# Attention over a graph on one core: PE's semaphores raised by drains instead of matmuls, ScalarE's copies in mid-chain with immediate biases, one-hots behind messages, and gathers up to 14 steps ahead

## The chip, the cores and the metric

The kernel runs on one core of one Trainium2 chip. The metric is the device time of one execution in microseconds (us). The engines are PE (TensorE, matmuls and their weight loads), DVE (VectorE), ACT (ScalarE), POOL (GpSimd, which here issues gathers) and SP (SyncE, which issues the large loads and the stores).

## The reference

One layer of graph attention with a residual and a layer norm. There are 6250 nodes with 128 features, 206250 edges (sorted by receiver) with 128 features each, and 4 heads of 32.

```python
sent  = nodes[senders] @ Ws + Ws_b
e_att = sent + edges @ We + We_b                      # (E, 4, 32)
recv  = nodes[receivers] @ Wr + Wr_b
logits = mish(e_att + recv) @ attn_w + attn_b         # (E, 4)
w = exp(logits - segment_max(logits, receivers)[receivers])
w = w / segment_sum(w, receivers)[receivers]
out = segment_sum(w * e_att, receivers)
x = layernorm(x + out)
```

## The kernel before

The node tables `nodes @ Ws` and `nodes @ Wr` are made first and written to DRAM. Then the edges are worked through in 51 windows of 4096 edges, 32 tiles of 128. A window has 8 groups of 4 tiles; the work on one group is called a step, so there are 408 steps. `run` writes two windows out, loops over pairs of windows, and ends with three more calls, so that each engine has its own fixed program, and only semaphores tie the engines to each other. Each window's softmax and sums are finished during the next two windows, beside those windows' own groups.

For group g of window w:

- POOL gathers the senders' rows of the table by four indirect DMAs (L717), each one tile of 128 rows. Ahead of a group it waits until PE has finished the products of the group `AHEAD` = 4 steps back (semaphore z_ps).
- DVE makes the one-hot matrix of the receivers (`one_hots`, L1113), three steps ahead of the group's products. It waits until PE has finished the sums that read the same buffer two windows earlier (sum_ready).
- PE turns (transposes) the edge tiles (L793) and the one-hot tiles (L798) into PSUM, two steps ahead (`turn`). The last transpose of each kind raises edgeT_ps or onehotT_ps.
- ACT copies both to SBUF (`copy_edgeT` L907, `copy_onehotT` L914).
- PE multiplies (`products`, L815 and L816, 16 matmul records a group) into ps_z; the last one raises z_ps.
- DVE adds the gathered rows (`add_gathered`, L1122), giving Z.
- ACT runs a chain of five activations over Z (`bound` L923, then `ratio_step` L930, L933, L936, L939), each with its bias in a 128x1 tile. From it DVE makes mish times the attention weights, and reduces it to logits (`mish` L1129, `score` L1138, `reduce_heads` L1144), one step later.
- In the window after, DVE finds the maxima over receivers and the weights, and multiplies Z by the weights (`messages`, L1205, at the steps in MSG_NEXT and MSG_LAST). PE sums the messages by receiver (`sums`, L827, 8 matmul records a group, at the steps in SUM_NEXT and SUM_LAST); the last matmul of a group raises sum_ready. Sums of group 0 wait until DVE has read the sums of the window before (att, L1224). `ends_to_row` (L835) and `maxima_back` (L842) are small transposes for the maxima, once a window each.

PE's order within a step is products, turn of the group two ahead, sums of the window before the last, the small transposes, and sums of the last window. ACT's is both copies, then the chain. DVE's is one-hots, Z, messages, and then mish, score and reduce with small operations between them (`aside`).

## Time and profile before

| | |
|---|---|
| median of 3 runs | 2656.48 us (2653.65 to 2662.03) |
| span of the profiled execution | 2661.8 us |
| PE busy | 1917.4 us, 72% |
| DVE busy | 1895.0 us, 71% |
| ACT busy | 1927.7 us, 72% |
| POOL busy | 1575.1 us, 59% |
| mean granted TensorE clock | 0.835 |

The span runs from the first to the last instruction of the profiled execution and is taken as that execution's time; no time of it around the span is on record, and it lies 0.2% above the median. Busy time is the time in which an engine executes; what it waits for is found in the list of waits and in the timelines. A releaser called "remote" is one that the profile can't name. "issue" is time in which the engine waited for nothing that the profile shows. PE's matmul ends are modelled, their starts are recorded. In a merged row of the timeline (x8) the time runs from the first start to the last end.

### The profile page before, as it was taken

The page shows a single profiled execution, that of the slowest core. Times are in us where ns is not written, and L with a number is a line of the kernel's source. Part 1 is how long each engine was busy: PE and PEld are TensorE (multiplying, and loading weights), DVE is VectorE, ACT ScalarE, POOL GpSimd, SP SyncE. Part 2 cuts the span into 40 slices and gives each one's busy share as a digit, 9 for nine tenths or more (in the row PEclk, how much of TensorE's full clock was granted, in tenths as well). Part 3 has the DMA queues.
Part 4 walks back from the last instruction along what each step waited for, and adds up shares of the span by engine and source line. Part 5 has one row for each costly group of instructions (what it writes and reads, how often), then busy time and mean ns, then how long its engine had stood idle before and what let it go on. Part 6 is the DMA issues. An engine that isn't in the chain of part 4 may idle for free.

```text
span 2661.8 us, 45397 instructions
## 1 busy us (share of the span) xinstructions
PE 1917.4 (72%) x13621; PEld 1789.2 (67%) x13621; DVE 1895.0 (71%) x3941; ACT 1927.7 (72%) x3126; POOL 1575.1 (59%) x1640
## 2 busy tenths in 40 slices
PE   5667777777776777776776777776777777776776
PEld 5567666766666776766666766666667676666665
DVE  2676777777777767776676777766777777677766
ACT  1777777777777777777777777777777777777774
POOL 2666656656666665666566656656666666556661
PEclk8888888888888887888888888878888888878877
DMA  6422322322232322232232232232223232223220
GB/s 191 130 77 80 105 83 78 112 79 77 81 111 77 97 96 77 77 113 79 76 112 79 78 105 86 78 100 90 78 93 99 79 98 95 77 86 104 79 79 17
DMA packets 106714, 240.18 MB, mean 90 GB/s; under 512 B 45800, under 2 KB 72546, under 8 KB 99658
## 3 DMA queue, kind: packets, MB, share of 16 engines
q1 hardware_dynamic: 53334, 132.54, 14.6%
q0 software_dynamic: 52224, 107.06, 14.1%
q10 hardware_dynamic: 1128, 0.25, 0.0%
q8 instruction: 13, 0.21, 0.0%
q14 instruction: 15, 0.12, 0.0%
HBM read 229.98 MB, written 9.74 MB: 90 GB/s over the span
## 4 chain that ended last, share of the span: by engine, by line
DVE 36%; PE 20%; another core or an unknown queue 18%; issue 17%; ACT 7%; DVEq 1%; DMA 1%; ACTq 0%; SPq 0%
PE ps_sum L827 7%; DVE Z L1122 6%; DVE tbuf L1138 6%; DVE tbuf L1129 6%; DVE Z L1205 5%; PE ps_z L815 4%; PE ps_z L816 4%; DVE onehot L1113 4%; DVE logit L1144 2%; PE ps_edgeT L793 2%; ACT tbuf L933 1%; ACT tbuf L930 1%; ACT tbuf L936 1%; ACT tbuf L923 1%
## 5 line engine op out<-in xcount | busy, mean ns | idle before, releaser
L717 POOL DMA_INDIRECT landing<-xs_table,src_i x1632 | 1574.2, 965 | 1034.1 <-issue 448.3
L815 PE MATMUL ps_z<-we_sb,edgeT 128*128 128x128 f32 x3264 | 767.2, 320 | 83.3 <-issue 82.4
L816 PE MATMUL ps_z<-xr_buf,onehotT 128*128 128x128 f32 x3264 | 751.9, 315 | 72.3 <-issue 71.5
L827 PE MATMUL ps_sum<-Z,onehot 128*128 128x132 f32 x3264 | 558.9, 321 | 204.7 <-DVE att L1224 95.2
L815 PEld LDWEIGHTS ps_z<-we_sb,edgeT 128*128 128x128 f32 x3264 | 613.0, 232 | 100.9 <-issue 97.3
L816 PEld LDWEIGHTS ps_z<-xr_buf,onehotT 128*128 128x128 f32 x3264 | 609.4, 231 | 83.1 <-issue 82.8
L827 PEld LDWEIGHTS ps_sum<-Z,onehot 128*128 128x128 f32 x3264 | 485.6, 224 | 223.8 <-issue 149.4
L1113 DVE TENSOR_TENSOR onehot<-iota_f,ps_dve 128x512 f32<-128x512 f32 x408 | 276.0, 677 | 432.5 <-remote 352.6
L923 ACT ACTIVATE tbuf<-Z,c_zmax 128x512 f32<-128x512 f32 x408 | 296.2, 726 | 165.7 <-DVE Z L1122 85.9
L907 ACT COPY edgeT<-ps_edgeT 128x512 f32<-128x512 f32 x408 | 235.3, 577 | 229.4 <-remote 179.9
L798 PE MATMUL ps_onehotT<-ident_half,onehot 128*128 128x128 bf16 x1632 | 176.6, 232 | 241.8 <-issue 103.8
L1122 DVE TENSOR_TENSOR Z<-ps_z,landing 128x512 f32<-128x512 f32 x408 | 278.5, 683 | 88.6 <-remote 72.9
L914 ACT CAST onehotT<-ps_onehotT 128x512 f32<-128x512 bf16 x408 | 238.8, 585 | 132.9 <-remote 120.5
L798 PEld LDWEIGHTS ps_onehotT<-ident_half,onehot 128*128 128x128 bf16 x1632 | 125.0, 104 | 291.3 <-issue 226.7
L930 ACT ACTIVATE tbuf<-tbuf,c_zmax 128x512 f32<-128x512 f32 x408 | 294.7, 722 | 13.3
L793 PE MATMUL ps_edgeT<-ident,landing 128*128 128x128 f32 x1632 | 281.1, 295 | 32.3 <-issue 31.9
L933 ACT ACTIVATE tbuf<-tbuf,c_one 128x512 f32<-128x512 f32 x408 | 294.6, 722 | 13.3
L936 ACT ACTIVATE tbuf<-tbuf,c_one 128x512 f32<-128x512 f32 x408 | 294.5, 722 | 13.3
L939 ACT ACTIVATE tbuf<-tbuf,c_ln 128x512 f32<-128x512 f32 x408 | 294.0, 721 | 11.6
L1129 DVE SCALAR_TENSOR_TENSOR tbuf<-tbuf,Z 128x512 f32<-128x512 f32 x408 | 279.3, 685 | 26.6 <-ACT tbuf L939 21.2
L1138 DVE TENSOR_TENSOR tbuf<-tbuf,ps_dve 128x512 f32<-128x512 f32 x408 | 278.4, 682 | 9.0
L1144 DVE TENSOR_REDUCE logit<-tbuf 128x16 f32<-128x512 f32 x408 | 277.9, 681 | 7.3
(110 smaller groups left out, 1228.3 us busy)
## 6 DMA issues: line engine op xcount, KB each, us to landing
landing<-in_edge_attr_dram SPq DMA_DIRECT2D x51, 2048.0 KB
landing<-xs_table,src_i POOLq DMA_INDIRECT x1632
x_in<-in_x_dram SPq DMA_DIRECT2D x51, 64.0 KB
xr_in<-xr_table SPq DMA_DIRECT2D x51, 64.0 KB
out_dram<-y_out SPq DMA_DIRECT2D x51, 64.0 KB
xr_buf<-xr_table SPq DMA_DIRECT2D x50, 64.0 KB
xs_table<-onehot SPq DMA_DIRECT2D x2, 896.0 KB
xr_table<-landing SPq DMA_DIRECT2D x1, 1568.0 KB
```

Source lines behind the costliest of these rows:

```text
L717: nc.gpsimd.indirect_dma_start(gath[b][:, t, :], None, xs_dram, bass.IndirectOffsetOnAxis(ap=src_i[:, b, t:t + 1], axis=0))\
L793: tr = nc.tensor.transpose(ps_edgeT[g % 2][:, j, :], edge_buf[:, b, a + j, :], ident[:, :])
L815: nc.tensor.matmul(ps_z[q][:, j, :], edgeT[:, q, j, :], we_sb[:, :], start=True, stop=False)
L816: mm = nc.tensor.matmul(ps_z[q][:, j, :], onehotT[:, q, j, :], xr_buf[:, b, :], start=False, stop=True)
L827: mm = nc.tensor.matmul(ps_sum[:, 0:ZC], OHv[:, b, t, :], Zv[:, b, t, :], start=(t == 0), stop=(t == T - 1))
L923: nc.scalar.activation(tb, Zv[:, b, a:a + n, 0:D], ACT.Relu, bias=c_zmax[:, 0:1], scale=-1.0)\
L930: nc.scalar.activation(tb, tb, ACT.Exp, bias=c_zmax[:, 0:1], scale=-1.0).then_inc(exp_done, 1)
L1113: nc.vector.tensor_tensor(OHv[:, b, a:a + n, :], iota_f[:, :].unsqueeze(1).to_broadcast([P, n, P]), local[:, b, a:a + n].unsqueeze(2).to_b ...
L1122: nc.vector.tensor_tensor(Zv[:, b, a:a + n, 0:D], ps_z[g % 2][:, 0:n, :], gath[b][:, a:a + n, :], ALU.add).then_inc(z_ready, 1)
L1129: nc.vector.scalar_tensor_tensor(out=tb, in0=tb, scalar=1.0, in1=Zv[:, b, a:a + n, 0:D], op0=ALU.subtract, op1=ALU.mult, reverse0=True)\
L1138: nc.vector.tensor_tensor(tb, tb, row.to_broadcast([P, n, D]), ALU.mult).then_inc(scored, 1)
L1144: nc.vector.tensor_reduce(logit[:, b, :, a:a + n].rearrange("p h t -> p t h"), tb, AX.X, ALU.add)\
```

## The change

PE's matmuls in the windows no longer raise semaphores. After the products of a group and all sums of that step PE executes a drain, and this raises z_ps; sum_ready is raised behind it. Then PE turns the pieces of the group two ahead, and a second drain raises one semaphore, turned_ps, in place of edgeT_ps and onehotT_ps. The small transposes have a drain of their own. The sums thus stand ahead of the turned pieces, and the groups 0 and 1 of the last window are summed in step 5, group 2 in step 6 and group 3 in step 7. ACT does both copies in one place, the one-hots first, behind the third operation of its chain instead of ahead of the first. The activations' biases are immediates instead of 128x1 tiles, and the tile c_zmax is gone. DVE makes its one-hots after Z and the messages of a step instead of first. POOL may gather 14 steps ahead instead of 4. SP waits for turned_ps where it waited for edgeT_ps.

```diff
-AHEAD = 4
+AHEAD = 14
...
-SUM_NEXT = {5: [0], 6: [1], 7: [2, 3]}
+SUM_NEXT = {5: [0, 1], 6: [2], 7: [3]}
...
-                wait_apart(sp, edgeT_ps, at(w - 2, NG - 1), past_sp)
+                wait_apart(sp, turned_ps, at(w - 2, NG - 1), past_sp)
...
                 if g == 0:
                     pe.wait_ge(edge_landed[b], k * 16 + 16)
-                wait(pe, edgeT_ready, at(w, g) - 2)
                 for j in range(n):
-                    tr = nc.tensor.transpose(ps_edgeT[g % 2][:, j, :], edge_buf[:, b, a + j, :], ident[:, :])
-                tr.then_inc(edgeT_ps, 1)
+                    nc.tensor.transpose(ps_edgeT[g % 2][:, j, :], edge_buf[:, b, a + j, :], ident[:, :])
                 pe.wait_ge(onehot_ready, at(w, g))
                 wait(pe, onehotT_ready, at(w, g) - 1)
...
-                tr.then_inc(onehotT_ps, 1)
+                return tr
...
-                mm.then_inc(z_ps, 1)
+                return mm
...
-                mm.then_inc(sum_ready, 1)
+                return mm
...
                 for g in range(NG):
                     if there(w):
                         products(w, b, k, g)
+                    last = SUM_LAST.get(g, []) if there(w - 2) else []
+                    for m in last:
+                        sums(w - 2, b, m)
+                    coming = SUM_NEXT.get(g, []) if there(w - 1) else []
+                    for m in coming:
+                        sums(w - 1, 1 - b, m)
+                    if there(w):
+                        pe.drain().then_inc(z_ps, 1)
+                    elif last or coming:
+                        pe.drain()
+                    if last or coming:
+                        pe.sem_inc(sum_ready, len(last) + len(coming))
                     w1, b1, g1 = two_after(w, b, g)
                     if there(w1) and there(w):
                         turn(w1, b1, k if w1 is w else (k + b if b else k), g1)
-                    for m in SUM_LAST.get(g, []) if there(w - 2) else []:
-                        sums(w - 2, b, m)
+                        pe.drain().then_inc(turned_ps, 1)
...
                     if g == 1 and there(w - 1):
                         ends_to_row(w - 1, 1 - b)
+                        pe.drain().then_inc(ends_ps, 1)
                     if g == 3 and there(w - 1):
                         maxima_back(w - 1)
-                    for m in SUM_NEXT.get(g, []) if there(w - 1) else []:
-                        sums(w - 1, 1 - b, m)
+                        pe.drain().then_inc(back_ps, 1)
...
+            def copy_turned(w, b, g):
+
                 n = GROUPS[g][1]
                 q = g % 2
...
+                act.wait_ge(turned_ps, at(w, g))
                 wait(act, z_ps, at(w, g) - 2)
                 nc.scalar.copy(onehotT[:, q, 0:n, :], ps_onehotT[:, 0:n, :].bitcast(BF16)[:, :, 0:P])\
                     .then_inc(onehotT_ready, 1)
+                nc.scalar.copy(edgeT[:, q, 0:n, :], ps_edgeT[q][:, 0:n, :]).then_inc(edgeT_ready, 1)
...
-                nc.scalar.activation(tb, Zv[:, b, a:a + n, 0:D], ACT.Relu, bias=c_zmax[:, 0:1], scale=-1.0)\
+                nc.scalar.activation(tb, Zv[:, b, a:a + n, 0:D], ACT.Relu, bias=ZMAX, scale=-1.0)\
...
-                    nc.scalar.activation(tb, tb, ACT.Square, bias=c_one[:, 0:1]).then_inc(sq_done, 1)
+                    nc.scalar.activation(tb, tb, ACT.Square, bias=1.0).then_inc(sq_done, 1)
...
-                    if coming:
-                        copy_edgeT(w1, b1, g1)
-                        copy_onehotT(w1, b1, g1)
                     if here:
                         bound(w, b, g)
                         ratio_step(w, g, 0)
                         ratio_step(w, g, 1)
+                    if coming:
+                        copy_turned(w1, b1, g1)
...
-                    if there(w1) and there(w):
-                        one_hots(w1, b1, g1)
                     if there(w):
                         add_gathered(w, b, k, g)
                     if g == 4 and there(w - 1):
                         weights_near(w - 1, 1 - b)
                     all_messages(w, b, g)
+                    if there(w1) and there(w):
+                        one_hots(w1, b1, g1)
```

## Rows read from the trace of the kernel before

**Rows 1.** The page: span, busy time by engine, and the gathers' group (mean ns).

```profile
span 2661.8 us, 45397 instructions
...
PE 1917.4 (72%) x13621; PEld 1789.2 (67%) x13621; DVE 1895.0 (71%) x3941; ACT 1927.7 (72%) x3126; POOL 1575.1 (59%) x1640
...
L717 POOL DMA_INDIRECT landing<-xs_table,src_i x1632 | 1574.2, 965 | 1034.1 <-issue 448.3
```

**Rows 2.** The waits: engine, line, releaser: us in total, times, longest.

```profile
POOL landing L717 <- remote: 364.1, 147, 3.4
DVE onehot L1113 <- remote: 352.6, 104, 9.5
...
POOL landing L717 <- PE ps_z L816: 185.0, 80, 15.4
```

**Rows 3.** The timeline, DVE and PE: steps 4 to 6 of a window, and mid-chain.

```profile
1202.07 0.68 DVE L1122 TENSOR_TENSOR Z<-ps_z,landing 128x512 f32<-128x512 f32 x1
...
1207.05 0.28 DVE L1224 TENSOR_TENSOR att<-ps_sum,rden 128x128 f32<-128x128 f32 x1
...
1207.99 0.17 DVE L1095 TENSOR_SCALAR far<-dst_i 128x32 f32<-128x32 int32 x1
...
1213.13 1.12 PE L827 MATMUL ps_sum<-Z,onehot 128*128 128x132 f32 x8
...
1214.09 0.38 PE L815 MATMUL ps_z<-we_sb,edgeT 128*128 128x128 f32 x2
...
1220.98 0.69 DVE L1113 TENSOR_TENSOR onehot<-iota_f,ps_dve 128x512 f32<-128x512 f32 x1 [6.15 <-remote]
...
1239.31 0.27 PE L816 MATMUL ps_z<-xr_buf,onehotT 128*128 128x128 f32 x1 [2.42 <-issue]
```

**Rows 4.** The timeline of POOL's gathers, and one wait of DVE.

```profile
38.35 1.11 POOL L717 DMA_INDIRECT landing<-xs_table,src_i  x1 [36.61 <-DMA xs_table<-onehot]
...
73.63 0.94 POOL L717 DMA_INDIRECT landing<-xs_table,src_i  x1 [15.45 <-PE ps_z L816]
...
1218.25 0.94 POOL L717 DMA_INDIRECT landing<-xs_table,src_i  x1 [0.30 <-issue]
...
1327.07 0.94 POOL L717 DMA_INDIRECT landing<-xs_table,src_i  x1 [0.30 <-issue]
...
1329.82 0.69 DVE L1113 TENSOR_TENSOR onehot<-iota_f,ps_dve 128x512 f32<-128x512 f32 x1 [6.39 <-remote]
...
2609.04 0.95 POOL L717 DMA_INDIRECT landing<-xs_table,src_i  x1 [0.30 <-issue]
```

**Rows 5.** The timeline of one step without a stall: DVE, PE and weight loads.

```profile
1225.90 0.68 DVE L1122 TENSOR_TENSOR Z<-ps_z,landing 128x512 f32<-128x512 f32 x1
...
1228.68 0.30 PEld L815 LDWEIGHTS ps_z<-we_sb,edgeT 128*128 128x128 f32 x2
...
1228.79 0.38 PE L815 MATMUL ps_z<-we_sb,edgeT 128*128 128x128 f32 x2
...
1229.98 0.68 DVE L1122 TENSOR_TENSOR Z<-ps_z,landing 128x512 f32<-128x512 f32 x1
```

**Rows 6.** Busy time by stretch; after the busy times come granted clock, DMA, GB/s.

```profile
1100.00:1600.00 500.00, 362.30 (x2593) 337.67 (x2592) 359.92 (x747) 369.26 (x602) 305.23 (x316) 0.84 0.28 89
```

**Rows 7.** Groups: busy us, mean ns, idle before; PE's large ones, two of ACT's.

```profile
L815 PE MATMUL ps_z<-we_sb,edgeT 128*128 128x128 f32 x3264 | 767.2, 320 | 83.3 <-issue 82.4
L816 PE MATMUL ps_z<-xr_buf,onehotT 128*128 128x128 f32 x3264 | 751.9, 315 | 72.3 <-issue 71.5
L827 PE MATMUL ps_sum<-Z,onehot 128*128 128x132 f32 x3264 | 558.9, 321 | 204.7 <-DVE att L1224 95.2 <-issue 93.8 <-DVE Z L1205 9.6
L793 PE MATMUL ps_edgeT<-ident,landing 128*128 128x128 f32 x1632 | 281.1, 295 | 32.3 <-issue 31.9
...
L956 ACT ACTIVATE lnv<-mv,c_eps 128x1 f32<-128x1 f32 x51 | 14.3, 280 | 14.7 <-DVE mv L1242 14.7
L958 ACT ACTIVATE rstd<-lnv 128x1 f32<-128x1 f32 x51 | 10.3, 203 | 1.6
```

More of the change, by code:

```diff
@@ L55 @@
 NLATER = 3
-VCONST = 12
-IOTAS = 11
+VCONST = 11
 SEARCH = 3
@@ L157, in gat_kernel @@
         c_eps = sb("c_eps", [P, 1])
-        c_zmax = sb("c_zmax", [P, 1])
         ones = sb("ones", [P, 1])
@@ L257, in gat_kernel @@
         onehot_ready = sem("onehot_ready")
-        edgeT_ps = sem("edgeT_ps")
-        onehotT_ps = sem("onehotT_ps")
+        turned_ps = sem("turned_ps")
         edgeT_ready = sem("edgeT_ready")
@@ L835, in ends_to_row @@
                     tr = nc.tensor.transpose(ps_ends[0:H, c * P:(c + 1) * P], ends, ident[:, :])
-                tr.then_inc(ends_ps, 1)
+                return tr
             def maxima_back(w):
@@ L842, in maxima_back @@
                     tr = nc.tensor.transpose(ps_ends[:, c * H:(c + 1) * H], im[:, c, :], ident[0:H, 0:H])
-                tr.then_inc(back_ps, 1)
+                return tr
             def window(w, b, k):
@@ L857, in window @@
                         ends_to_row(w - 1, 1 - b)
+                        pe.drain().then_inc(ends_ps, 1)
                     if g == 3 and there(w - 1):
                         maxima_back(w - 1)
-                    for m in SUM_NEXT.get(g, []) if there(w - 1) else []:
-                        sums(w - 1, 1 - b, m)
+                        pe.drain().then_inc(back_ps, 1)
             pe.wait_ge(s_xs, 2 * NB)
-            turn(0, 0, 0, 0)
-            turn(0, 0, 0, 1)
+            for g in range(2):
+                turn(0, 0, 0, g)
+                pe.drain().then_inc(turned_ps, 1)
             run(pe, window)
@@ L900, in _ @@
             act.wait_ge(s_vconst, VCONST)
-            def copy_edgeT(w, b, g):
+            def copy_turned(w, b, g):
                 n = GROUPS[g][1]
                 q = g % 2
-                act.wait_ge(edgeT_ps, at(w, g))
-                wait(act, z_ps, at(w, g) - 2)
-                nc.scalar.copy(edgeT[:, q, 0:n, :], ps_edgeT[q][:, 0:n, :]).then_inc(edgeT_ready, 1)
-            def copy_onehotT(w, b, g):
-                n = GROUPS[g][1]
-                q = g % 2
-                act.wait_ge(onehotT_ps, at(w, g))
+                act.wait_ge(turned_ps, at(w, g))
                 wait(act, z_ps, at(w, g) - 2)
@@ L929, in ratio_step @@
                     act.wait_ge(bounded, at(w, g))
-                    nc.scalar.activation(tb, tb, ACT.Exp, bias=c_zmax[:, 0:1], scale=-1.0).then_inc(exp_done, 1)
+                    nc.scalar.activation(tb, tb, ACT.Exp, bias=ZMAX, scale=-1.0).then_inc(exp_done, 1)
                 elif k == 1:
                     act.wait_ge(exp_done, at(w, g))
-                    nc.scalar.activation(tb, tb, ACT.Square, bias=c_one[:, 0:1]).then_inc(sq_done, 1)
+                    nc.scalar.activation(tb, tb, ACT.Square, bias=1.0).then_inc(sq_done, 1)
                 elif k == 2:
                     act.wait_ge(sq_done, at(w, g))
-                    nc.scalar.activation(tb, tb, ACT.Ln, bias=c_one[:, 0:1]).then_inc(ln_done, 1)
+                    nc.scalar.activation(tb, tb, ACT.Ln, bias=1.0).then_inc(ln_done, 1)
                 else:
                     act.wait_ge(ln_done, at(w, g))
-                    nc.scalar.activation(tb, tb, ACT.Exp, bias=c_ln2[:, 0:1], scale=-1.0).then_inc(ratio_ready, 1)
+                    nc.scalar.activation(tb, tb, ACT.Exp, bias=LN2, scale=-1.0).then_inc(ratio_ready, 1)
             def items(w):
@@ L982, in _ @@
             for g in range(2):
-                copy_edgeT(0, 0, g)
-                copy_onehotT(0, 0, g)
+                copy_turned(0, 0, g)
             run(act, window)
@@ L993, in _ @@
             nc.vector.memset(c_eps[:, :], EPS).then_inc(s_vconst, 1)
-            nc.vector.memset(c_zmax[:, :], ZMAX).then_inc(s_vconst, 1)
             nc.vector.memset(ones[:, :], 1.0).then_inc(s_vconst, 1)
```

## Prediction

> **What bounds the kernel now.** I read the page first, then the list of waits, then the timelines of a stalled stretch and of a smooth one, then the groups of PE and ScalarE. The page shows no engine at its limit: DVE, ScalarE and PE lie near 72%, GpSimd at 59% [rows 1]. The span of 2661.8 us holds 408 steps (51 windows of 8), so a step takes about 6.3 us, and no engine has that much work: DVE 1895.0/408 = 4.64 us, ScalarE 1927.7/408 = 4.72 us, and GpSimd four gathers of 965 ns with 0.30 us between two of them [rows 1, 4], 5.06 us. So the order of the work bounds it, not a rate.
>
> The list of waits says which order. The longest ones end at "remote", a releaser that the profile can't place: GpSimd's gathers 364.1 us and DVE's one-hots 352.6 [rows 2]; ScalarE's copies follow. On one core there is no other core. What each of these instructions waits for is, by the code, a semaphore raised by PE's last matmul of a group. The stalled stretch shows it: PE's group of sums starts at 1213.13 and lasts 1.12, the products behind it start at 1214.09; yet the one-hots that wait for sum_ready start at 1220.98, after 6.15 us idle [rows 3]. The signal came some 6 us after the work. When nothing is late, one DVE step takes 1229.98 - 1225.90 = 4.08 us [rows 5].
>
> When are signals late? Between 1218 and 1330 us DVE's one-hots have four such waits. In the first GpSimd's last gather ended at 1219.19 and DVE was let go at 1220.98; in the last they are 1328.01 and 1329.82: 1.8 us after the gathers had stopped both times [rows 3, 4]. GpSimd had stopped because it waits for z_ps, a signal of the same kind. I read this as: signals attached to matmuls are held up while gathers are being issued. That is argued from these places, not shown.
>
> **The change, part by part.**
>
> *The drains.* No matmul of the windows raises a semaphore any more; a drain does, after products with sums, and after the turned pieces. If the drain's signal is prompt, the "remote" waits go. What then sets the time? First GpSimd: it starts at 38.35 and issues 1632 gathers at 965 + 300 ns, the last of them at 38.35 + 1631 x 1.265 = 2101.6; from the last gather's start to the end lie 2661.8 - 2609.04 = 52.8 us [rows 1, 4]. That floor is 2154 us. Second PE: a step has 32 matmuls, 16 of products, 8 of sums, 8 of turned pieces, at 0.11 us from start to start (two in 0.38 us where one lasts 0.27 [rows 3, 5]), 3.52 us, at the mean granted clock of 0.84 [rows 6] 4.19 us. Its idle time put down to "issue" on the four large lines is 82.4 + 71.5 + 93.8 + 31.9 = 280 us [rows 7], 0.69 us a step. The trace has no drain between matmuls. From below, an empty PE costs the last matmul's tail and the next weight load: a lone matmul lasts 0.27 us against 0.11 of spacing, and a load takes 0.19 (two in 0.30) [rows 3, 5], so 0.16 + 0.19 = 0.35 us. From above, a drain waits as long as a late signal does, 3.4 us on average (352.6/104 [rows 2]). I take the lower value, since PE went on starting matmuls while its signal was out, and only the signal is seen to be late. Two drains: 0.70 us. PE's step is then 4.19 + 0.69 + 0.70 = 5.58 us; times 408 = 2277 us, with 73 us up to the first products (they release GpSimd at 73.63 [rows 4]) and 53 behind, 2403 us. This counts every slow-clock stretch of today, while PE should wait less than today.
>
> The Trainium skill (PSUM — Partial Sum Buffer, Engine vs sequencer instructions) tells to attach the increment to the matmul, and says of a drain that it "waits for the engine to go fully idle". By that rule the change gives away PE's overlap twice a step. The trace has no such drain to agree with.
>
> *Sums before the z_ps signal, regrouped.* Z of a step with sums now waits one to two groups of 8 matmuls (0.9 to 1.8 us) longer. DVE has other work until then, but not in the step with groups 0 and 1 (step 5): group 0 waits for att, which DVE makes 5.3 us after Z of step 4 (1202.07 to 1207.33 [rows 3]); two groups and a drain later, 1.8 + 0.35, z_ps comes at 1209.5, where DVE is free at 1208.2. So 1.3 us a window of DVE idle, 3.1 at half clock: 65 to 160 us of DVE in all. Against 5.06 us per step of GpSimd, DVE has 0.42 spare, 3.4 us a window, so it lies beside the gathers as long as these run ahead. Without that cover it costs its 65 to 160 us. What is late next there: the turned pieces of step 7, whose copies ScalarE reaches only behind three activations. SP's load of edges waits for the same drain, under 1 us later, for pieces needed six steps on: nothing.
>
> *ScalarE.* The two copies move from the head of the step behind three activations, so bound starts sooner by both, and PE gets its pieces three activations later, with two steps of lead: nothing by itself. Five activations a step lose their bias tile. With one 128x1 input, ln with a bias tile takes 280 ns and exp without takes 203 [rows 7]: 77 ns, times 5 times 408 = 157 us of ScalarE's busy time, between nothing (if it is the function's difference) and that. ScalarE falls to some 4.34 us a step, and as it was no bound, it gives slack only.
>
> The Trainium skill (ScalarE: Activation LUTs, What ACT_TABLE_LOAD costs) gives about 93 ns for each pointer operand. By it the sum would be 190 us, an estimate from that page; the row's 77 ns is on its side.
>
> *One-hots behind messages.* Three steps ahead as before; 0.6 to 1.9 us later in the step, and PE needs them one step on. Z starts 0.6 us sooner. Nothing is queued behind a late one-hot but mish of the step before, whose ratio is ready later anyway. *Gather lead 14.* Gathers now wait for a step 14 back, so GpSimd stops only for sender indices, which SP loads about two windows ahead. Alone it takes 549 us of GpSimd's waits for z_ps (364.1 + 185.0 [rows 2]) away, which cost nothing now unless Z waits for a landing.
>
> **The sum.** Between GpSimd's 2154 and PE's 2403 I take 2300 us: above the middle (2279), as window edges and step 5 cost a little on either bound, below PE's own sum since the clock should be higher. The page's execution took 2661.8, the median of the runs shown is 2656.48, 0.2% less; 2300 stands for both.
>
> **The rivals.** *Forecast: signals prompt, step 5.0 to 5.8 us.* For it: the stalls hang on signals, not on work, and the "remote" waits are all for PE's. Against: the cause of the delay isn't seen. 2154 to 2450 us, chance 0.62.
>
> *PE becomes the bound and eats most of it.* Drains of 0.5 us: 4.88 + 1.0 = 5.88 us a step, 2399 + 126 = 2525 us. For it, PE stands in mid-chain without a wait for 2.42 us at 1239.31 [rows 3], which no drain mends. Chance 0.13, 2450 to 2640.
>
> *Slower: the hold is on the matmuls' completion, not on the signal.* Then a drain waits for it, PE stands instead of running ahead, and lead 14 removes the pauses in the gathers after which the hold ended. With the 1.8 us of the stalls per drain a step is 4.88 + 3.6 = 8.5 us, some 3590 us. It decides from 0.72 us a drain, where 4.88 + 1.44 is today's 6.3. For it: all stalls ended after a pause. Against: matmuls kept starting every 0.11 us while the signal was out (products from 1214.09 [rows 3]), so results were moving. Chance 0.22.
>
> The Trainium skill (SBUF — State Buffer, Who interferes with whom) has it that PE waits on no one and that DMA doesn't contend with engines. By it the gathers would not be the cause and the lead harmless. The stalls speak against it, without proof.
>
> *No change:* signals stay late but no more often, the lead hides it. 2650 to 2665, chance 0.03.
>
> **How the numbers follow.** No change means within 0.3%, about what a measurement of this kernel can tell. Faster is 0.62 + 0.13 = 0.75, same 0.03, slower 0.22. The range starts at the gather floor, 2150, and reaches to 2700: the forecast, PE as the bound, no change and a few of the slower cases, 0.8 together. The likeliest case's own range is 2154 to 2450.
>
> **What the profile after would show.** Right: hardly any "remote" wait, under 150 us in all; GpSimd's busy share over 68% with waits for z_ps gone; Z to Z 5.0 to 5.8 us; ScalarE's activations 77 ns shorter; a new wait of DVE's Z or one-hots on a drain in step 5. Wrong in size: PE idle behind drains far over 0.35 us. Wrong in kind: PE stands 2 us or more at drains while gathers run, and spans over 2700 us. If the activations' mean does not fall, the bias tile was free.

## The result and the profile after

The change makes the kernel slower: 3011.48 us median of 5 runs (2971.54 to 3027.1) against 2653.65 us (2652.18 to 2662.03), a ratio of 1.1285 with a 95% interval of 1.1249 to 1.132. The ratio and its interval are taken from three of the five, since the two at 3022.11 and 3027.1 us lie over 1.5% above the fastest; the medians alone would give 1.135. The prediction was 2300 us. The profiled execution took 2971.54 us; its span is 2969.7, and that is what the rows below are measured against.

The page of the kernel after: span, busy time by engine, the gathers' group.

```profile
span 2969.7 us, 46325 instructions
...
PE 1958.3 (66%) x13621; PEld 1776.1 (60%) x13621; DVE 1908.4 (64%) x3940; ACT 1711.0 (58%) x3126; POOL 1625.5 (55%) x1640
...
L714 POOL DMA_INDIRECT landing<-xs_table,src_i x1632 | 1624.6, 995 | 1237.3 <-PEq L853 728.9 <-issue 446.4 <-DMA xs_table<-onehot 35.5
```

All engines do about the same work as in [rows 1], ScalarE less, and all have more idle time. GpSimd's waits for PE have grown: PEq L853 is the first drain, the one that raises z_ps.

The list of waits of the kernel after (us in total, times, longest):

```profile
ACT tbuf L927 <- DVE Z L1123: 856.2, 348, 20.6
DVE Z L1123 <- PEq L853: 807.6, 327, 28.7
POOL landing L714 <- PEq L853: 728.9, 292, 9.3
...
PE ps_edgeT L790 <- issue: 420.3, 364, 20.4
PE ps_z L811 <- issue: 349.7, 386, 20.3
```

The waits for "remote" of [rows 2] are gone from the top of the list, as forecast. What stands there is one chain: ScalarE waits for Z, Z waits for the first drain. And PE itself now has idle time of which it had little: 420.3 us ahead of the turned pieces (behind the first drain), where it was 31.9 [rows 7], and 349.7 ahead of the products (behind the second, in some steps behind that of the small transposes), where it was 82.4. The profile shows no semaphore that PE waits for there; I read it as standing in its drain. That is 770 us for the 816 drains of 408 steps, 0.94 us each.

The mean hides two kinds. Counted over the timeline of the whole execution, the two rows are 750 stands: 424 of them last 0.30 us or less, and 232 last over 1 us. These 232 make 610 of the 770 us, 2.6 us each.

The longest two, on PE's timeline at the start of the work:

```profile
112.37 0.63 PE L812 MATMUL ps_z<-xr_buf,onehotT 128*128 128x128 f32 x2
133.42 1.11 PE L790 MATMUL ps_edgeT<-ident,landing 128*128 128x128 f32 x4 [20.41 <-issue]
134.32 0.63 PE L794 MATMUL ps_onehotT<-ident_half,onehot 128*128 128x128 bf16 x4
155.29 0.77 PE L811 MATMUL ps_z<-we_sb,edgeT 128*128 128x128 f32 x2 [20.34 <-issue]
```

The matmuls are over at 113.0; PE starts the next ones 20.41 us later, and after them it stands for 20.34 us again. GpSimd's timeline in that stretch, first and last of its gathers:

```profile
103.61 0.94 POOL L714 DMA_INDIRECT landing<-xs_table,src_i  x1 [26.53 <-DMA src_i<-in_src_dram]
104.86 0.94 POOL L714 DMA_INDIRECT landing<-xs_table,src_i  x1 [0.31 <-issue]
...
157.62 0.94 POOL L714 DMA_INDIRECT landing<-xs_table,src_i  x1 [0.30 <-issue]
166.44 0.94 POOL L714 DMA_INDIRECT landing<-xs_table,src_i  x1 [7.88 <-PEq L853]
```

With a lead of 14 it gathers for 55 us without a pause, and PE hardly works meanwhile. Both stands end while the gathers go on (no pause of theirs is over 0.31 us from 104.86 to 158.56). The table by stretch shows how little PE does and the granted clock (columns as in [rows 6]):

```profile
60.00:200.00 140.00, 55.10 (x325) 48.25 (x326) 48.88 (x91) 45.92 (x82) 76.65 (x81) 0.65 0.29 91
109.00:113.00 4.00, 3.44 (x16) 3.19 (x16) 2.95 (x5) 3.73 (x8) 3.09 (x4) 0.61 0.26 70
155.00:159.00 4.00, 3.71 (x16) 3.49 (x16) 0.00 (x0) 2.23 (x4) 2.83 (x3) 0.50 0.18 49
1100.00:1600.00 500.00, 344.36 (x2362) 313.47 (x2363) 332.71 (x686) 300.35 (x550) 288.42 (x289) 0.84 0.26 81
```

From 60 to 200 us PE is busy for 55 of 140 us, at a granted clock of 0.65. Behind the second stand it works at 0.50, the lower of its two levels, but ahead of the first stand it was already down to 0.61. From 1100 to 1600 us the clock is 0.84, as in [rows 6], but there are 2362 matmuls where there were 2593. The timeline of DVE there shows the step:

```profile
1404.54 0.69 DVE L1123 TENSOR_TENSOR Z<-ps_z,landing 128x512 f32<-128x512 f32 x1 [2.79 <-PEq L853]
...
1410.14 0.65 DVE L1123 TENSOR_TENSOR Z<-ps_z,landing 128x512 f32<-128x512 f32 x1
...
1417.07 0.69 DVE L1123 TENSOR_TENSOR Z<-ps_z,landing 128x512 f32<-128x512 f32 x1 [0.85 <-PEq L853]
...
1423.86 0.69 DVE L1123 TENSOR_TENSOR Z<-ps_z,landing 128x512 f32<-128x512 f32 x1 [1.18 <-PEq L853]
```

Three steps in 19.32 us, 6.4 us each in this stretch, where the forecast was 5.0 to 5.8; over the whole span, less the prediction's 126 us at its two ends, it is (2969.7 - 126)/408 = 6.97.

### The profile page after: what moved, and what is told of

It reads as the page before. It is cut to its first block, busy times and chain, and to the rows that moved or that the text cites. A ratio compares the mean times of both kernels' runs of the same rounds, so it can differ in the third digit from the quotient of the medians.

```text
span 2969.7 us, 46325 instructions
## 1 busy us (share of the span) xinstructions
PE 1958.3 (66%) x13621; PEld 1776.1 (60%) x13621; DVE 1908.4 (64%) x3940; ACT 1711.0 (58%) x3126; POOL 1625.5 (55%) x1640
## 3 DMA queue, kind: packets, MB, share of 16 engines
q1 hardware_dynamic: 53334, 132.54, 12.9%
## 4 chain that ended last, share of the span: by engine, by line
PEld 50%; issue 36%; PEldq 8%; DVE 3%; another core or an unknown queue 1%; PE 1%; ACT 1%; DMA 1%; SPq 0%; DVEq 0%; ACTq 0%
PEld ps_z L812 15%; PEld ps_z L811 14%; PEld ps_sum L823 13%; PEld ps_edgeT L790 4%; PEldq L853 3%; PEld ps_onehotT L794 3%; PEldq L861 1%; PEldq L291 1%; PE ps_z L751 1%; PEldq L857 1%; DVE Z L1206 1%; DVE tbuf L1130 0%; DVE onehot L1114 0%; PEld ps_ends L838 0%
## 5 line engine op out<-in xcount | busy, mean ns | idle before, releaser
L714 POOL DMA_INDIRECT landing<-xs_table,src_i x1632 | 1624.6, 995 | 1237.3 <-PEq L853 728.9
L811 PE MATMUL ps_z<-we_sb,edgeT 128*128 128x128 f32 x3264 | 806.4, 336 | 372.7 <-issue 349.7
L927 ACT ACTIVATE tbuf<-Z 128x512 f32<-128x512 f32 x408 | 257.1, 630 | 915.3 <-DVE Z L1123 856.2
L812 PE MATMUL ps_z<-xr_buf,onehotT 128*128 128x128 f32 x3264 | 768.0, 324 | 0.0
L812 PEld LDWEIGHTS ps_z<-xr_buf,onehotT 128*128 128x128 f32 x3264 | 630.8, 240 | 0.0
L790 PE MATMUL ps_edgeT<-ident,landing 128*128 128x128 f32 x1632 | 279.8, 298 | 423.8 <-issue 420.3
L823 PE MATMUL ps_sum<-Z,onehot 128*128 128x132 f32 x3264 | 471.8, 294 | 52.5 <-DVE ps_ends L1221 32.7
L790 PEld LDWEIGHTS ps_edgeT<-ident,landing 128*128 128x128 f32 x1632 | 184.1, 149 | 498.0 <-issue 497.9
L823 PEld LDWEIGHTS ps_sum<-Z,onehot 128*128 128x128 f32 x3264 | 442.6, 210 | 61.4 <-issue 31.0
L1206 DVE TENSOR_TENSOR Z<-Z,ps_dve 128x512 f32<-128x512 f32 x408 | 272.4, 679 | 2.0 <-issue 0.2
L937 ACT ACTIVATE tbuf<-tbuf 128x512 f32<-128x512 f32 x408 | 257.1, 630 | 12.9
L934 ACT ACTIVATE tbuf<-tbuf 128x512 f32<-128x512 f32 x408 | 257.1, 630 | 12.9
L943 ACT ACTIVATE tbuf<-tbuf 128x512 f32<-128x512 f32 x408 | 256.3, 628 | 11.3
L940 ACT ACTIVATE tbuf<-tbuf 128x512 f32<-128x512 f32 x408 | 261.8, 642 | 0.1
```

What stands on the lines that cost most here:

```text
L714: nc.gpsimd.indirect_dma_start(gath[b][:, t, :], None, xs_dram, bass.IndirectOffsetOnAxis(ap=src_i[:, b, t:t + 1], axis=0))\
L790: nc.tensor.transpose(ps_edgeT[g % 2][:, j, :], edge_buf[:, b, a + j, :], ident[:, :])
L811: nc.tensor.matmul(ps_z[q][:, j, :], edgeT[:, q, j, :], we_sb[:, :], start=True, stop=False)
L812: mm = nc.tensor.matmul(ps_z[q][:, j, :], onehotT[:, q, j, :], xr_buf[:, b, :], start=False, stop=True)
L823: mm = nc.tensor.matmul(ps_sum[:, 0:ZC], OHv[:, b, t, :], Zv[:, b, t, :], start=(t == 0), stop=(t == T - 1))
L940: nc.scalar.activation(tb, tb, ACT.Ln, bias=1.0).then_inc(ln_done, 1)
```

## The experiments

The kernels ran in five groups, each on one chip with the kernel before beside them. The kernel before did not take the same time in all groups. The chip numbers on record are 11 for A and D, 0 for B and E, and 14 for C. Ratios are to the kernel before of the same group:

| group | kernel before, us | kernel: median us, ratio, 95% interval |
|---|---|---|
| A | 2654.89 | after_signals_on_matmuls: 2737.04, 1.0309 (1.0276 to 1.0341) |
| | | after_lead_4: 2941.43, 1.1069 (1.1034 to 1.1105) |
| B | 2172.54 | before_few_gathers: 2064.55, 0.9501 (0.9477 to 0.9526) |
| | | after_few_gathers: 2227.43, 1.0247 (1.0221 to 1.0273) |
| | | before_lead_14: 2172.01, 0.9998 (0.9988 to 1.0009) |
| | | before_immediate_biases: 2173.32, 1.0005 (0.9991 to 1.0018) |
| C | 2606.98 | after_again: 2934.81, 1.1273 (1.1222 to 1.1323) |
| | | before_two_drains: 2841.35, 1.0894 (1.0824 to 1.0963) |
| | | before_no_gathers: 2093.71, 0.8017 (0.7986 to 0.8048) |
| | | after_no_gathers: 2294.63, 0.8802 (0.8769 to 0.8834) |
| D | 2650.48 | before_lead_14_again: 2790.27, 1.0523 (1.0493 to 1.0554) |
| | | before_spaced_gathers: 2920.25, 1.099 (1.0942 to 1.1038) |
| | | after_signals_on_matmuls_no_gathers: 2070.02, 0.7814 (0.7789 to 0.7838) |
| | | before_two_drains_no_gathers: 2132.78, 0.8045 (0.8018 to 0.8072) |
| E | 2652.95 | after_signals_lead_4: 2655.43, 1.0009 (0.999 to 1.0028) |
| | | after_signals_lead_2: 2652.49, 0.9995 (0.9981 to 1.0009) |
| | | before_gathers_in_eights: 2687.9, 1.0118 (1.0083 to 1.0154) |
| | | before_lead_2: 2643.57, 0.9965 (0.9948 to 0.9983) |

**The drains.** after_signals_on_matmuls is the changed kernel with its semaphores on the matmuls again:

```diff
-                        products(w, b, k, g)
+                        products(w, b, k, g).then_inc(z_ps, 1)
...
-                        sums(w - 1, 1 - b, m)
-                    if there(w):
-                        pe.drain().then_inc(z_ps, 1)
-                    elif last or coming:
-                        pe.drain()
-                    if last or coming:
-                        pe.sem_inc(sum_ready, len(last) + len(coming))
+                        sums(w - 1, 1 - b, m).then_inc(sum_ready, 1)
...
-                        turn(w1, b1, k if w1 is w else (k + b if b else k), g1)
-                        pe.drain().then_inc(turned_ps, 1)
+                        turn(w1, b1, k if w1 is w else (k + b if b else k), g1).then_inc(turned_ps, 1)
```

> The changed kernel with its order, biases and lead, but each semaphore raised by the last matmul of its group again and no drain. Completion theory (while gathers are issued, PE's matmuls are not taken as complete, and a drain makes PE stand until they are): PE runs ahead again while signals are late, 2450 to 2650 us. Drain-cost theory (a drain costs PE its tail and refill, gathers or not): the same 2450 to 2650. Order theory (z_ps behind the sums, copies in mid-chain, one-hots late are what costs): stays at 2900 to 3050.

It took 2737.04, outside every range that I gave: drains and what goes with them are worth 9.8 of the 12.9%, but 3.1% stay. This edit moves more than the drains: z_ps is raised by the products again, so it comes ahead of the sums and not behind them. It can't tell the two apart. after_lead_4 is the changed kernel with `AHEAD = 4`:

> The changed kernel with gathers 4 steps ahead instead of 14. Completion theory: GpSimd stands at its lead in both, one group of gathers for each z_ps, so within 1% of the changed kernel, 2960 to 3050 us. Pause theory (lead 14 took the pauses away in which holds end): back to 2650 to 2850.

It took 2941.43, between my two ranges: the lead of 14 is worth some 2% beside the drains. The reverse edit, before_two_drains, is the old order and the old lead with drains alone, one right behind the products and one behind the turned pieces; the sums keep their semaphore on a matmul:

```diff
-                tr.then_inc(edgeT_ps, 1)
...
-                tr.then_inc(onehotT_ps, 1)
+                pe.drain().then_inc(onehotT_ps, 1)
+                pe.sem_inc(edgeT_ps, 1)
...
-                mm.then_inc(z_ps, 1)
+                pe.drain().then_inc(z_ps, 1)
```

> The kernel before in its own order, lead 4, with two drains a step in place of semaphores on matmuls: one behind the products raises z_ps, one behind the turned one-hots raises onehotT_ps and edgeT_ps. The sums keep theirs. Theory A (the drains cost it): where the kernel before takes 2655, this takes 2850 to 2950, most of the loss of the whole change, since after_signals_on_matmuls, which has all but the drains, lost only 3.1%; where it takes 2173, 1 to 4% slower. Rival B (the order with sums ahead of the turned pieces costs it, since the drain waits behind more matmuls): within 2% of the kernel before on either chip.

> The changed kernel unaltered, beside the other runs of this call, on whichever chip they get. Two chips have been seen: on one the kernel before took 2655 us and its matmuls' semaphores came late, on the other it took 2173 us and no semaphore came late. Theory A (the two drains a step let PE stand until its matmuls are counted as done, and that takes long only where gathers hold it): where the kernel before takes 2655, this takes 2970 to 3030 with drains that end 1.5 us and more late; where the kernel before takes 2173, this takes 2280 to 2400, a ratio of 1.05 to 1.10, by PE's bare drains and the sums' wait for att in step 5. Rival B (the order, not the drains, makes it slow): the ratio is 1.13 on either chip.

Drains alone: +8.9%; all of the change in the same group: +12.7%. Both ratios are as theory A had them, and rival B of before_two_drains (within 2%) is out. So the drains carry most of the loss. The timeline of PE in before_two_drains shows one drain behind the turned one-hots:

```profile
1213.08 0.39 PE L797 MATMUL ps_onehotT<-ident_half,onehot 128*128 128x128 bf16 x4
1218.57 2.12 PE L827 MATMUL ps_sum<-Z,onehot 128*128 128x132 f32 x8 [5.11 <-issue]
```

PE stands for 5.11 us, and the profile shows nothing that it waits for, where in [rows 3] the products started while the signal was out. I call this the hold: while it lasts, a signal on a matmul is late but PE goes on, and a drain makes PE itself stand. That fits matmuls whose completion is held. One reading is left beside it, that PE's signals are held and a drain waits for its own signal to go out. No run has a drain without a signal, so this stays open; for the time of a kernel with drains the two come to the same.

**Are gathers the cause?** before_few_gathers and after_few_gathers leave out three of each group's four gathers from the third window on; before_no_gathers and after_no_gathers leave out all of them from there. DVE then adds rows that were gathered earlier, so these kernels do less than the whole work and don't compute the result. (A form without three quarters of the gathers from the first window on, before_quarter_gathers and after_quarter_gathers, has no time on record.)

```diff
+                few = 4 if isinstance(w, int) and w < 2 else 0
...
-                    for t in range(a, a + n):
+                    for t in range(a, a + few):
...
-                dve.wait_ge(gath_landed[b][g], k * (16 * n) + 16 * n)
+                dve.wait_ge(gath_landed[b][g], k * 0 + 64)
```

With one gather left of four, the `else 0` is `else 1`, and `k * 0` is `k * 16`. SP's wait for the same semaphore is adapted in the same way.

> The kernel before; from the third window on only one of the four gathers of each group is issued, and three quarters of the senders' rows are left from the first windows. Completion theory: the late signals go with the gathers, 2100 to 2350 us, and waits for remote releasers fall under 150 us. If something else than gathers holds PE's signals: 2600 to 2660, waits unchanged.

> The changed kernel with the same gathers left out. Completion theory: drains become short and the kernel takes 2200 to 2450 us. Drain-cost theory (a drain costs PE 0.6 us or more of tail and refill, gathers or not): 2800 to 3000. Order theory (z_ps behind the sums and late copies): likewise 2800 or more.

> Leaves the senders' gathers out from the third window on (DVE adds what lies there from the first two windows); all else as in the kernel before. Theory A (GpSimd's gathers hold PE's completions): with no gathers running no semaphore of PE comes late on any chip, and it takes 2000 to 2080 us on either, a gain of 22 to 25% where the kernel before takes 2655 and of 4 to 8% where it takes 2173. Rival C (something else of that chip holds them, such as DMA traffic as a whole or the clock): where the kernel before takes 2655, the late semaphores stay, over 200 us of waits for a releaser that the profile can't place, and it gains under 10%.

> The changed kernel with the same gathers left out. Theory A: with no gathers the drains end 0.1 to 0.4 us behind the last matmul, and it takes 2180 to 2260 us on either chip, 6 to 10% above before_no_gathers, which is the price of two bare drains and of the order. Rival C: on a chip where the kernel before takes 2655, drains still end 1.5 us and more late, and it takes over 2700.

The runs with few gathers fell into group B, in which the kernel before took 2172.54 us. They took 2064.55, a little under its range, and 2227.43, in its range, but they can't speak on the hold, for there was none to remove: in the list of waits of before_lead_14, of the same group, none of the large ones ends at "remote", and from its first gather on GpSimd never waits longer than 0.3 us behind one: it gathers for some 2094 us without a pause, and nothing is held. These are two of its rows.

```profile
POOL landing L717 <- issue: 485.5, 1593, 0.3
...
DVE Z L1122 <- DMA landing<-xs_table,src_i: 141.0, 53, 4.3
```

The runs without gathers fell into group C, with the hold. before_no_gathers is 513 us faster than the kernel before, 20% (I had expected 22 to 25%, and 2000 to 2080 us); its page and the top of its list of waits:

```profile
PE 1650.8 (79%) x13621; PEld 1566.2 (75%) x13621; DVE 1878.8 (90%) x3941; ACT 1896.1 (90%) x3126; POOL 63.6 (3%) x72
...
PE ps_onehotT L800 <- ACT onehotT L916: 176.4, 198, 7.5
```

Of waits for "remote" 46.5 us are left in all, the largest group 18.7 us ahead of Z, and DVE and ScalarE are the bound at 90%. Rival C wanted over 200 us of such waits and a gain under 10%. So taking out the gathers takes out the hold. Whether it is GpSimd's work of issuing them or the transfers themselves isn't told apart: no run moved the same rows from another queue.

after_no_gathers, list of waits:

```profile
DVE Z L1125 <- PEq L855: 264.9, 171, 26.0
...
PE ps_z L813 <- issue: 118.3, 353, 8.4
PE ps_edgeT L792 <- issue: 110.0, 346, 20.8
```

PE's idle time behind drains has fallen from 770 to 228 us, and of its 699 stands 592 last 0.30 us or less and 3 over 1 us. But the changed kernel took more than the 2180 to 2260 us that I expected: it is still 9.6% above before_no_gathers (2294.63 to 2093.71), and in group B after_few_gathers is 7.9% above before_few_gathers. So part of the loss has nothing to do with the hold. Two runs divide it.

> The changed kernel without its drains (semaphores on the matmuls again) and without the senders' gathers from the third window on. It tells what is left in after_no_gathers of the order and what of bare drains: before_no_gathers took 2094, after_no_gathers 2295. Theory A: bare drains are 0.35 us each and lie on the chain from products to Z, so most of the 201 us is theirs, and this takes 2090 to 2160. Rival: the order (sums ahead of turned pieces, copies in mid-chain) has it, and this takes over 2230.

> The kernel before with the two drains a step and without the senders' gathers from the third window on. Theory A: 2100 to 2180, since PE has 0.7 us more a step but is not the bound without holds (its busy share was 79%); the gap between this and before_two_drains at 2841 is what held completions cost when PE stands for them. Rival (a drain costs over 0.5 us even with nothing held): over 2230.

Without gathers: old order 2094, old order with two drains 2133, new order 2070, new order with its drains 2295 (2094 and 2295 are of group C, 2133 and 2070 of group D, whose kernels before differ by 1.7%). Across the groups the drains cost 39 us in the old order and some 225 in the new one. A difference between the groups of 1.7%, some 35 us, could move both, so the first may be anything from nothing to 75 us; that the second is several times as large stands. before_two_drains_no_gathers fell into its expected range, after_signals_on_matmuls_no_gathers a little below its own. What no expectation said is that two drains cost so much more in the new order. The timelines of after_no_gathers show where. This is step 5, PE and then DVE:

```profile
1190.17 3.55 PE L825 MATMUL ps_sum<-Z,onehot 128*128 128x132 f32 x16 [3.15 <-DVE att L1227]
...
1193.78 0.69 DVE L1125 TENSOR_TENSOR Z<-ps_z,landing 128x512 f32<-128x512 f32 x1 [2.83 <-PEq L855]
```

In this step the sums of groups 0 and 1 wait 3.15 us for att, and the drain that raises z_ps stands behind them, so Z waits too. Summed over the timeline, Z's waits ahead of step 5 are 157.1 us of its 264.9 in after_no_gathers, and 149.4 of 231.7 in after_few_gathers. In the three other kernels without gathers they are 3.4, 6.3 and 19.7 us, each in a single wait. Two steps later in the same stretch the sums wait for nothing, and Z waits less:

```profile
1206.01 0.39 PE L814 MATMUL ps_z<-xr_buf,onehotT 128*128 128x128 f32 x2
...
1206.24 1.07 PE L825 MATMUL ps_sum<-Z,onehot 128*128 128x132 f32 x8
...
1207.36 0.69 DVE L1125 TENSOR_TENSOR Z<-ps_z,landing 128x512 f32<-128x512 f32 x1 [0.75 <-PEq L855]
...
1207.54 0.63 PE L792 MATMUL ps_edgeT<-ident,landing 128*128 128x128 f32 x4 [0.23 <-issue]
...
1208.62 0.46 PE L813 MATMUL ps_z<-we_sb,edgeT 128*128 128x128 f32 x2 [0.23 <-issue]
```

The products end at 1206.40, but Z starts at 1207.36, after DVE has been idle for 0.75 us: it waits out the sums, because one drain stands behind both. In the old order with drains z_ps has its own drain right behind the products. This is read from the traces; a run with the new order and a drain of its own right behind the products wasn't made. The same rows give the bare drain: the next matmul starts 0.23 us after the last one's end, and by the modelled ends a matmul ends 0.16 us after the next could start, 0.39 us.

**The lead and the pattern of the gathers.** before_lead_14 and before_lead_14_again are the kernel before with `AHEAD = 14`.

> The kernel before with gathers 14 steps ahead, nothing else. Completion theory: a stretch of gathers without pause near the start holds PE, then GpSimd stands at its lead again as before: 2670 to 2730 us. If the lead alone is harmless, as the prediction had it: 2648 to 2662.

> The kernel before with a gather lead of 14 alone, once more, since the first such run was on a chip that showed no hold. Theory A (gathers without a pause hold PE's completions): on a chip where the kernel before takes over 2600, the longer lead takes pauses away and makes the late semaphores more frequent, but it also keeps Z from waiting for rows: within 3% either way, with the longest single waits at the start (20 us, as in the profile of the changed kernel). Rival (the lead is what costs the changed kernel its time): 6% slower or more.

Nothing without the hold (0.9998, in group B, where the completion theory's 2670 to 2730 us could not be tried), 5.2% with it. My expectation of within 3% was too low, and the rival's 6% too high. The list of waits of before_lead_14_again:

```profile
DVE onehot L1113 <- remote: 472.4, 99, 13.6
...
POOL landing L717 <- remote: 337.1, 130, 7.9
...
POOL landing L717 <- DMA src_i<-in_src_dram: 181.0, 32, 24.8
```

DVE's one-hots wait 472.4 us for late signals where it was 352.6 [rows 2], the longest 13.6 where it was 9.5. GpSimd pauses about as often as before (227 pauses of over 0.6 us, where it was 243), but part of them now comes where sender indices are late, up to 24.8 us, and in between it runs on for longer: 23 stretches of gathers last over 15 us without a pause, where it was 4. before_spaced_gathers spreads the four gathers of a group over a step, before_gathers_in_eights lets eight run and then waits, before_lead_2 has `AHEAD = 2`:

```diff
                     for t in range(a, a + n):
+                        if t > a and (not isinstance(w, int) or at(w, g) > AHEAD):
+                            wait_apart(pool, (exp_done, sq_done, ln_done)[t - a - 1], at(w, g) - AHEAD, past_pool)
```

```diff
-                    if not isinstance(w, int) or at(w, g) > AHEAD:
+                    if g % 2 == 0 and (not isinstance(w, int) or at(w, g) > AHEAD):
```

> The kernel before with the four gathers of a group spread over a step: the first waits for PE's products four steps back as before, the second, third and fourth wait for ScalarE's second, third and fourth operation of the step four back. Theory A in the form that the time without a pause of 2.6 us decides: spaced gathers still leave no long pause, semaphores are as late as before or later, and it is 0 to 5% slower. Rival form (only gathers right behind each other hold them): with a pause of 0.3 us more behind each gather the late semaphores go, and it takes 2200 to 2450 us where the kernel before takes 2600.

> The kernel before with GpSimd's wait for PE's products at every second group only, so that eight gathers run and a pause of twice the length follows. Long runs without a pause hold completions longer (10 us), long pauses free them surely. Theory A: since a step needs a signal of PE several times, the longer run costs more than the longer pause gives, 2 to 8% slower. Rival (long pauses are what heals, as 9.9% lost by spreading the gathers suggests): 2 to 8% faster.

> The kernel before with a lead of 2. The lead of 14 lost 5.2%. If pauses decide, 0 to 3% faster; if rows come too late for Z, slower by 2% or more, with a wait of Z for landings of over 200 us.

Spreading loses 9.9%, twice what I gave it at most, so a little room between gathers does not help (GpSimd also waits for ScalarE there, which may be part of it). Late signals grew with it; these are ScalarE's copies, which waited 179.9 us for "remote" in the kernel before:

```profile
ACT edgeT L909 <- remote: 432.5, 108, 6.5
```

Eights lose 1.2%, less than expected; a lead of 2 gains 0.35%. The order fits one reading, that the hold ends in pauses of the gathers and comes while they run. The traces speak for it too. In the kernel before, 91 of DVE's 104 late one-hots start in a pause, 81 of them 1.4 to 2.2 us after the last gather's end, where the prediction had read 1.8 at two places. In the changed kernel, 162 of the 232 stands of over 1 us end in a pause. But 70 end while gathers go on, the two of 20 us among them, so pauses are not all that ends a hold. And since GpSimd mostly pauses because it waits for PE itself, these counts show what goes together, not which is the cause; that the gathers are, is shown by leaving them out.

**What is left of the change.** after_signals_lead_4 is after_signals_on_matmuls with `AHEAD = 4`, after_signals_lead_2 with 2, before_immediate_biases the kernel before with immediates.

```diff
-                nc.scalar.activation(tb, Zv[:, b, a:a + n, 0:D], ACT.Relu, bias=c_zmax[:, 0:1], scale=-1.0)\
+                nc.scalar.activation(tb, Zv[:, b, a:a + n, 0:D], ACT.Relu, bias=ZMAX, scale=-1.0)\
...
-                    nc.scalar.activation(tb, tb, ACT.Square, bias=c_one[:, 0:1]).then_inc(sq_done, 1)
+                    nc.scalar.activation(tb, tb, ACT.Square, bias=1.0).then_inc(sq_done, 1)
```

> The changed kernel without its drains and with the lead back at 4: what is left is the order of PE, ScalarE and DVE and the immediate biases. after_signals_on_matmuls (lead 14) lost 3.1%, and the lead of 14 alone cost the kernel before 5.2% on the same chip. If the lead's price adds up, this is 1 to 3% faster than the kernel before (2580 to 2630 us where that takes 2655). Rival (the order itself costs 3% where completions are held, since the sums stand ahead of the turned pieces): 2 to 4% slower.

> The same with a lead of 2. If late completions follow from gathers that run without a pause, a shorter lead ties GpSimd closer to PE and adds pauses: 0 to 3% faster than with a lead of 4. Rival (rows come too late for Z): slower than with a lead of 4 by 2% or more, with a wait of Z for landings of over 200 us.

> The kernel before with the five biases as immediates, nothing else. ScalarE's activations fall from 722 to near 630 ns. Slack theory (ScalarE is off the path): within 0.5% of before. If ScalarE's chain is on the path in the steps without a late signal: 2580 to 2640 us.

The order with immediate biases is worth nothing either way where the hold is on (1.0009), so the 3.1% of after_signals_on_matmuls were the lead's. The gain of 1 to 3% that I expected by taking 5.2% off 3.1% did not come: the parts don't add up like that. Nor did a lead of 2 gain over one of 4 (2652.49 to 2655.43). The immediates do make ScalarE faster. The group of the second activation, in before_immediate_biases and then in before_lead_14 of the same group:

```profile
L930 ACT ACTIVATE tbuf<-tbuf 128x512 f32<-128x512 f32 x408 | 257.3, 631 | 13.0
```

```profile
L930 ACT ACTIVATE tbuf<-tbuf,c_zmax 128x512 f32<-128x512 f32 x408 | 294.7, 722 | 13.3
```

91 ns each, and the time is the same (1.0005). That is group B, without the hold; with it the immediates ran only together with the new order.

## Why the prediction was wrong

**The step that failed** is the choice between the two bounds of the drain: "I take the lower value, since PE went on starting matmuls while its signal was out, and only the signal is seen to be late." The runs show that this does not follow: in before_two_drains, with nothing but the drains changed, PE stood for 5.11 us at such a place, and in the changed kernel 232 stands last over 1 us, 2.6 us on average, where the prediction had 0.35 for every drain. Over all drains it is 0.94 us of idle time and 0.16 of tail, and drains alone cost 8.9%. Of the rivals the one that had it was "the hold is on the matmuls' completion, not on the signal", at 0.22.

**That rival's price was off; that PE stands was right.** Whether it is the completion that is held, as the rival has it, or PE's signals with the drain behind them, no run tells. It put 1.8 us on each drain and came to 3590 us. That was taken from how long stalls went on after the gathers had stopped; measured are 1.10 us a drain, tail included. With these its own sum gives 4.88 + 2 x 1.10 = 7.08 us a step, times 408 and 126 beside, 3015 us, against 2971.54 in the profiled run and 3011.48 in the median. That it comes so near is in part luck: the 4.88 already holds 0.28 us of idle time a step on the same two lines (82.4 + 31.9 [rows 7]); without these it gives 2900 us. The point from which it decided, 0.72 us, was passed.

**The bare drain** was sized well: 0.35 against 0.39 us.

**Step 5** was seen and sized, at 65 to 160 us of DVE idle, and then covered by the gathers. The traces have 157.1 and 149.4 us of it in the two changed kernels with gathers left out, and 164.7 in the changed kernel. The size was right, at its upper end. Its cover was worth nothing as it came: in the changed kernel it is GpSimd that waits for PE, 728.9 us, and not the reverse. With gathers left out, the new order with drains is 7.9 to 9.6% slower than the old one, and most of Z's waits for the first drain are this term.

**2300 us as a time for prompt drains** was not far off: the changed kernel took 2227.43 and 2294.63 us with gathers left out. What it missed is that the kernel before, with prompt signals, takes 2172.54 us with all its gathers. So where nothing is held the change is a loss too, by after_few_gathers of at least 2.5%, an estimate; the forecast set what it takes without the hold against a kernel before that has it.

**GpSimd's floor** of 2154 us was sound as a floor: in group B the kernel before comes to 2172.54 with its gathers 0.3 us apart. Prompt signals go with 18% less time there (2172.54 to the 2652.95 of group E), and no drain was needed for it.

**Lead 14** was costed at nothing in the sum, and in the rival as taking the pauses away. The rival had it: 5.2% alone, 2% beside the drains (1.1285 and 1.1273 against 1.1069). GpSimd's waits for z_ps did not go either, they rose from 549 us to 728.9, since PE got later.

**A reading was off by one:** between 1218 and 1330 us five of DVE's one-hots wait for "remote", not four. Nothing hangs on it.

**ScalarE's 77 ns** measured 91, and as slack it gave nothing, as said. The Trainium skill (ScalarE: Activation LUTs, What ACT_TABLE_LOAD costs) was cited with about 93 ns; the runs are on its side.

**The one-hots' and copies' place** changed nothing that a run shows with the hold (1.0009). Without gathers the new order is 1.1% faster (2070 to 2094), less than the two groups differ by.

**The rule that was weighed**, the Trainium skill (SBUF — State Buffer, Who interferes with whom), has PE waiting on no one. Without gathers the hold goes (tried in groups C and D), with them it is there, in four groups of five and in the runs of the result. There the measurement decides against the rule as the prediction used it, that the gathers could not be the cause; in group B the two agree.

**Not settled:** what in a gather makes the hold, whether it is on completions or on PE's signals, what differs between group B at 2173 us and the others above 2600 (B and E have the same chip number), and what the changed kernel itself takes where nothing is held: it didn't run there. after_few_gathers leaves work out, so it can only bound it from below, at 2227.43 us.

## What to carry to other kernels

When a signal is late but its engine goes on, don't take what the engine starts as proof that its work is completed: here a drain turned late signals into an engine that stands. Try one drain before all of them. A drain costs what stands ahead of it: put it right behind the work whose consumer waits, not behind work that nobody waits for. A lead that takes an issuing engine's pauses away is a change by itself; run it alone.

## What was not expected of the hardware

- The same kernel took 2172.54 us in group B (19 runs, 2168.76 to 2181.04) and 2652.95 in group E (25 runs, 2643.52 to 2661.58). What the traces show of it are PE's late signals: waits at "remote" of 352.6 and 364.1 us in the profile of [rows 2], a run of 2662 us, none among the large ones in before_lead_14 of group B.
- While gathers ran for 55 us on end, PE stood in two drains for 20.41 and 20.34 us. In group B they ran for some 2094 us on end and nothing was held.
- Spreading the four gathers of a group over a step made late signals more (432.5 us ahead of ScalarE's copies where it was 179.9) and the kernel 9.9% slower.
- Behind a stand of 20 us the granted clock was 0.50 (155 to 159 us), but it was down to 0.61 ahead of the first such stand (109 to 113 us), when PE had been idle for 0.63 and 1.52 us just before.
